# Moving the last wait of a scan-and-experts kernel from SyncE to GpSimd

## What is computed

```python
mod = (silu(c) @ wmod).reshape(32, 6, 1, -1)          # sa, ca, ga, sb, cb, gb; ga and gb kept away from 0
h = layernorm(x) * (1 + ca) + sa
g, a = sigmoid(h @ Wg.T + bg), sigmoid(h @ Wd.T + bd)
v = h @ Wv.T + bv
x = x + ga * (causal_scan((1 - a) * v, a) * g)        # s_t = a_t * s_(t-1) + (1 - a_t) * v_t
h = layernorm(x) * (1 + cb) + sb
gate = softmax(h @ gate_w.T + gate_b), only the best 2 of 8 experts kept
x = x + gb * sum_over_experts(gate * (relu(h @ w1 + b1) @ w2 + b2))
```

## Time and profile before

| | |
|---|---|
| median of 3 runs | 443.9 us (442.91 to 444.16) |
| profiled execution, its own time | 442.52 us |
| span of the profiled execution, first to last instruction | 440.7 us |
| busy share of the span | VectorE (DVE) 88%, TensorE (PE) 83%, ScalarE (ACT) 73%, GpSimd (POOL) 43% |
| mean granted TensorE clock | 0.922 |

### The profile page before, as it was taken

How to read it: one execution, slowest core, us unless ns; L and a number is a source line. 1 busy time by engine, 2 the same in 40 slices (tenths; PEclk the granted TensorE clock), 3 DMA queues, 4 the chain that set the end, 5 groups by cost and what they waited for, 6 DMA issues and landing times.

```text
span 440.7 us, 15289 instructions
## 1 busy us (share of the span) xinstructions
PE 366.2 (83%) x4679; PEld 316.8 (72%) x4680; DVE 386.4 (88%) x1099; ACT 320.0 (73%) x992; POOL 188.7 (43%) x213
## 2 busy tenths in 40 slices
PE   1859889789787683489999999999999999999660
PEld 1435555456455562489999999999999999989660
DVE  4989999989998999699999899999999998888660
ACT  1445999688979550188988888889888888877530
POOL 8023303376678477884333243333333334324321
PEclk9986999989999655599999999999999999999895
DMA  7813643131223243563333333333333333232200
GB/s 217 223 48 106 202 146 106 48 128 73 92 90 126 93 163 147 147 197 106 84 98 84 95 94 100 87 88 86 87 86 91 94 85 87 66 81 73 64 11 7
DMA packets 45941, 45.27 MB, mean 103 GB/s; under 512 B 5934, under 2 KB 40575, under 8 KB 45874
## 3 DMA queue, kind: packets, MB, share of 16 engines
q1 hardware_dynamic: 38208, 27.28, 23.1%
q0 software_dynamic: 6592, 16.92, 10.6%
q10 hardware_dynamic: 1074, 0.23, 0.3%
HBM read 24.52 MB, written 20.81 MB: 103 GB/s over the span
## 4 chain that ended last, share of the span: by engine, by line
PE 58%; DVE 27%; issue 8%; DMA 2%; ACT 1%; SPq 1%; POOL 0%; POOLq 0%; ACTq 0%; DVEq 0%
PE bank L1513 8%; PE bank L1514 8%; PE bank L1515 8%; PE bank L1530 8%; PE bank L1531 7%; PE bank L1529 7%; DVE xn L921 3%; PE bank L1526 2%; DVE hs L935 2%; PE bank L1488 2%; PE bank L1370 2%; DVE st L865 2%; DVE u L931 2%; DVE st L859 2%; DVE pay L944 2%
## 5 line engine op out<-in xcount | busy, mean ns | idle before, releaser
L755 ACT ACTIVATE xs<-bank,b1col 128x128 f32<-128x128 f32 x624 | 165.2, 415 | 26.4 <-PE bank L1515 25.5
L590 POOL DMA_INDIRECT out_dram<-tg,midx x78 | 81.9, 1049 | 150.9 <-DVE tg L1299 135.0
L1513 PE MATMUL bank<-xh,w1hi 128*128 128x128 f16 x624 | 109.9, 223 | 6.6 <-issue 3.7
L1529 PE MATMUL bank<-w2hi,xs 128*128 x624 | 112.7, 219 | 0.0
L1530 PE MATMUL bank<-w2hi,w2f 128*128 x624 | 112.6, 219 | 0.0
L1531 PE MATMUL bank<-w2lo,xs 128*128 x624 | 112.6, 219 | 0.0
L1515 PE MATMUL bank<-xh,w1lo 128*128 128x128 f16 x624 | 109.9, 222 | 0.0
L1514 PE MATMUL bank<-xl,w1hi 128*128 128x128 f16 x624 | 109.9, 223 | 0.0
L1279 DVE TENSOR_TENSOR w2f<-xs 128x1024 f16<-128x1024 f32 x78 | 95.6, 1225 | 2.7
L561 POOL DMA_INDIRECT sorted_rows<-pay,idx x64 | 69.1, 1080 | 28.2 <-issue 18.7
L1277 DVE CAST xs<-xs 128x1024 f16<-128x1024 f32 x78 | 54.7, 701 | 13.1 <-ACT xs L755 9.5
(11 more groups left out here) (232 smaller groups left out, 654.2 us busy)
## 6 DMA issues: line engine op xcount, KB each, us to landing
xs<-sorted_rows SPq DMA_DIRECT2D x78, 130.0 KB
xs<-sorted_rows SPq DMA_DIRECT2D x78, 64.0 KB
sorted_rows<-padt SPq DMA_DIRECT2D x5, 582.0 KB, 5.3
w2f<-in_L_ffn_w_dram SPq DMA_DIRECT2D x4, 512.0 KB, 3.9
xs<-in_L_ffn_w_dram SPq DMA_DIRECT2D x4, 512.0 KB, 3.8
xs<-in_L_attn_x_dram SPq DMA_DIRECT2D x3, 512.0 KB, 8.7
out_dram<-tg,midx POOLq DMA_INDIRECT x78
sorted_rows<-pay,idx POOLq DMA_INDIRECT x64, 2.7
```

Source lines behind the costliest of these rows:

```text
L590: pool.indirect_dma_start(out_rows, bass.IndirectOffsetOnAxis(midx[k][:, t:t + 1], 0), yout[k][:, t, :], None, bounds_check=TOK - 1, oob_i ...
L755: ins = act.activation(hf[e][:, cc, t * P:(t + 1) * P], bank[2 * e + cc // 2][:, o:o + P], ACT.Relu, bias=b1col[:, bass.ds(ex[t][e] * HC + ...
L1513: pe.matmul(o, whi, xh[n % 2][:, rows], start=True, stop=False)
L1529: pe.matmul(o, hh[n % 2][e][:, cc, rows], whi, start=False, stop=False)
```

## The change

The two waits leave SyncE's stream, and stand at the end of GpSimd's, behind its last write and ahead of its drain. The semaphores and the counts waited for are the same.

```diff
@@ -472,10 +472,6 @@
             for k in range(BUFS):
                 reload_y(before_last, BUFS + k)
             reload_y(last, BUFS)
-
-            for k in range(BUFS):
-                sp.wait_ge(written[k], turns * (16 * HALVES) + (1 - k) * (16 * HALVES))
-                sp.sem_inc(sp_turn, 1)
 
 
         @block.gpsimd
@@ -600,6 +596,9 @@
                 for k in range(BUFS):
                     write_tile(it, k)
             write_tile(turns, 0)
+            for k in range(BUFS):
+                pool.wait_ge(written[k], turns * (16 * HALVES) + (1 - k) * (16 * HALVES))
+                pool.sem_inc(pool_turn, 1)
```

## The result

The changed kernel takes 445.44 us (median of 22 runs, 442.75 to 448.66), the kernel before 443.37 us (median of 22 runs taken beside them, 440.48 to 445.8). The ratio is 1.0051, with a 95% interval of 1.003 to 1.0072: **slower by 2.3 us, between 1.3 and 3.2** (the medians are 2.1 us apart). Where an execution took over 1.5% longer than the fastest of its kernel, it counts in no ratio; that is one of the 11 with GpSimd waiting under a short drain, further down.

A forecast was written before the change was run, and what follows sets the result against it. GpSimd's closing drain alone was taken to set the end: 440.5 + 0.8 shift + 0.2 barrier gave a 441.5 us span, 443.3 as a profiled execution, and 444.7 us as median with 1.4 more; range 435.9 to 446.0 us.

The forecast's parts named there:

- What bounds the end: Program's end: GpSimd's drain alone sets it, running 10.83 us from 429.7 to 440.5 us.
- the first rival: GpSimd's closing drain: cheap once nothing is in flight, ending at 433.1, a gain of 7.4 us, 436.5 us; chance 0.34.
- The removed half: SyncE's end: two waits and a register operation taken away, worth nothing because GpSimd's drain covers them.
- The added half: GpSimd's end: register operation hidden, waits pass at 432.7 and 432.8, drain starts at 432.9; its end was only bounded.
- the middle of the two bounds: GpSimd's closing drain: its end shifts by +0.8 us, wrong by at most 0.7 on this mechanism.
- upper end: GpSimd's closing drain: a 9.1 us price paid whole after its last work, whatever the DMAs do; +1.5 us.
- The lower end: GpSimd's closing drain: first needs the writes to land, then pays the remaining 7.7 us; +0.1 us.
- the forecast: GpSimd's closing drain: a price paid in full, 443.4 to 446.0 us; chance 0.58, of it 0.15 slower, 0.43 within 0.3%.
- The first call that has to be loaded: GpSimd's closing drain: some 6 of its 9.1 us would be loading code, no wait for a DMA, giving +1.5 us.
- The whole 10.83 us as the drain's own work: GpSimd's closing drain: rival counting all from its start, so it ends 3.2 us later, 447.1 us; chance 0.06.

The follow-up runs named there:

- GpSimd waiting under a short drain: The changed kernel with one more GpSimd drain after turn 7, against the kernel before: 439.4 us, ratio 0.9919.
- the drain per tile: The kernel before with a GpSimd drain added at the head of each tile's write: 439.11 us, ratio 0.987.
- the drain in the middle: The kernel before with one more GpSimd drain between the two stages, after 64 scatters; that drain took 5.30 us, no total time given.

## Why the prediction was right, and where it was off

*What bounds the end.* Right: GpSimd's drain alone set it, and taking the drain away gave 1.9% (the interval of 1.2 to 2.6% holds the 7.4 us of the first rival's sum).

*The removed half.* Right: worth nothing. SyncE's drain moved to 416.9 (expected near 417.4), and the kernel without any wait ran as before.

*The added half.* The waits pass where expected, the register operation is hidden, and the drain starts 1.46 us behind the last DMA instruction (estimated 1.5). The term that failed is the one in which I took **the middle of the two bounds, +0.8 us, for the drain's shift**. Its upper end, a price that is paid whole from the drain's start, was measured: 9.06 us with the writes landed, 9.1 with writes in flight, a shift of 1.4 us. The lower end rested on the drain first waiting for the landing and then paying 7.7 us; it fell. A drain does hold until the writes have landed, as the drain per tile shows, but with 142 DMAs that wait of 1.3 us runs beside the price and not ahead of it. With the upper end the sum would have been 445.4, against 445.44 measured. That near agreement is partly luck, since the median before was taken as 443.9 and came to 443.37 in the longer series; the ratio is what counts, and 1.4 us, 0.3%, lies just inside its interval, at the lower end. In one point the upper end was wrong as well: it took the price as fixed, and the price goes by the number of DMAs. For this change that makes no difference, since both kernels issue 142.

The other 0.9 us of the measured 2.3 lies in no row of the program's end. What lies ahead of the end scatters by more: the last DMA instruction ends between 429.7 and 434.8 us in the six profiled executions whose streams are the same up to there. Much of that scatter goes with the mean granted clock: the changed kernel took 442.75 to 444.66 us in its 8 executions at 0.92 or more, and 444.7 to 448.66 in the 14 below. For the 22 executions of the kernel before that were taken beside it, no clock is on record, but 30 later ones, taken beside the experiments, have it. A straight line of time against clock, with one step between the two kernels, fitted to these 30 and the 22, puts the step at 1.4 us with a standard error of 0.25. By this estimate the change costs what it holds up the drain by, and the 0.9 us is a different mix of clocks and chance.

*The chances.* "Within 0.3%" got 0.45 and "slower" 0.21; the outcome was slower. The quarter of the forecast that I gave to its upper end was too small. That the result lies within 435.9 to 446.0 says little for the mechanism, since this range was made to hold the cheap drain too; the rows of line 98 decide.

*The cheap drain* (the first rival) was wrong as put, landed writes don't make a drain cheap, and yet it holds something: a drain is cheap, 34 ns, when another has gone before it and nothing was issued since. The Trainium skill, VectorE: DVE Perf Modes, section The DRAIN you can't avoid, gives about 12 ns on all 5 engines for the drains that the runtime puts around a kernel. The drains of line 98 belong to the program's own block, and GpSimd's is not of that size: 34 ns with nothing to clear away, 1.4 to 9.07 us behind its last DMA instruction otherwise.

*The first call that has to be loaded*, from the Trainium skill, GPSIMD Engine Reference, section Instruction dispatch, was cited for the upper end. The end came out there, but not for that reason: the drain in the middle would have paid for the loading, and the closing drain then still took 6.5 us.

*The whole 10.83 us as the drain's own work* fell: the drain that starts with nothing left to execute takes 9.06.

## What to carry to other kernels

Where GpSimd issues DMAs, look at its drain on the line of the program's end, which the chain of waits doesn't reach: it may set the end by itself. Nothing that may run beside such a drain should be put ahead of it; let another engine wait for the last writes, whose landing the drain then hides. If the drain's length matters, pay for it earlier, at a place where GpSimd waits long enough and no other engine waits for its writes, or end the program with semaphores that say that the output is written, and without that drain.

## What the runs showed of the hardware that I had not expected

A drain of GpSimd has a price by the number of DMAs that GpSimd issued since its last drain: 83 ns each for 46, 64, 78 and 96 of them (3.8, 5.3, 6.45 and 7.9 us), less for more (8.6 us for 124, 9.06 for 142), and 34 ns for none. The price doesn't depend on whether the last writes have landed, as far as 46 and 142 DMAs show it, and at the program's end nothing moves on the DMA queues for most of it. With few DMAs the landing counts instead: behind two writes each of 39 drains ends 0.12 us after they have landed. The 2.0 us behind 18 writes, of which 0.7 lie behind the landing, fit neither the 83 ns nor the landing alone; that stays open, as does the flattening above 96. What GpSimd does for each DMA in those 83 ns isn't seen in any row.
